# AdaLN transformer block: modulation rows computed for four partitions and repeated by DMA

## The reference

```python
mod = (_silu(L0_c) @ L0_wmod).reshape(4, 6, 1, -1)
sa, ca, ga, sb, cb, gb = (mod[:, 0], mod[:, 1], mod[:, 2], mod[:, 3], mod[:, 4], mod[:, 5])
ga = (2 * (ga >= 0) - 1) * jnp.maximum(jnp.abs(ga), 0.25)
gb = (2 * (gb >= 0) - 1) * jnp.maximum(jnp.abs(gb), 0.25)
h = _layernorm(x) * (1 + ca) + sa
x = x + ga * attention(h)          # 16 heads of 128, rope, capped scores, causal
h = _layernorm(x) * (1 + cb) + sb
x = x + gb * experts(h)            # 64 experts, top 6 in 3 of 8 groups, plus a shared one
```

## Time and profile before

| | us |
|---|---|
| median of 3 runs | 1132.64 |
| lowest and highest of the runs | 1129.94, 1132.98 |
| profiled execution, its own time | 1128.71 |
| span of its instructions | 1127.0 |
| TensorE busy in the span | 1030.5 (91%) |
| VectorE busy | 613.1 (54%) |
| ScalarE busy | 496.4 (44%) |
| GpSimd busy | 408.3 (36%) |

### The profile page before, as it was taken

The page is one execution under the profiler, slowest core; times in us unless marked ns, Lnnn a source line. Parts: engine busy times, 40 slices in busy tenths (PEclk is TensorE's granted clock), DMA queues, the critical chain, the costliest instruction groups (busy, mean ns, idle before and its releaser), DMA issues.

```text
span 1127.0 us, 17346 instructions
## 1 busy us (share of the span) xinstructions
PE 1030.5 (91%) x5813; PEld 857.0 (76%) x5813; DVE 613.1 (54%) x1424; ACT 496.4 (44%) x909; POOL 408.3 (36%) x598
## 2 busy tenths in 40 slices
PE   4999999999999999999999999999897887777774
PEld 3689989899899898998998998988564544444443
DVE  3575555657667757657865757674573211111116
ACT  1355555555555545555555565455321232223220
POOL 2232222223224555222546422265335244444440
PEclk9999999999999999999999999999999999999995
DMA  9970000001000110100101012000011598899966
GB/s 358 341 240 0 0 0 1 1 1 38 1 1 24 49 53 19 38 1 1 42 35 38 9 38 83 1 15 19 1 57 33 155 228 220 224 227 230 228 122 223
DMA packets 58752, 95.66 MB, mean 85 GB/s; under 512 B 7771, under 2 KB 41318, under 8 KB 58176
## 3 DMA queue, kind: packets, MB, share of 16 engines
q1 hardware_dynamic: 46880, 80.66, 22.4%
q0 software_dynamic: 11808, 14.16, 6.6%
HBM read 62.17 MB, written 40.67 MB: 91 GB/s over the span
## 4 chain that ended last, share of the span: by engine, by line
PE 76%; DMA 11%; DVE 7%; issue 2%; another core or an unknown queue 1%; ACT 1%; POOL 1%; SPq 1%; DVEq 0%; POOLq 0%; ACTq 0%
PE ps L1169 23%; PE ps L1216 12%; PE ps L1192 12%; PE ps L1205 10%; DMA wds<-in_wd 10%; PE ps L1382 5%; PE ps L1397 3%; PE ps L1178 2%; PE ps L1199 2%; PE ps L1181 2%; PE ps L1253 1%; PE ps L1328 1%; DMA css<-in_cossin 1%; PE ps L1150 1%
## 5 line engine op out<-in xcount | busy, mean ns | idle before, releaser
L395 POOL TENSOR_TENSOR holdp<-neghalf 128x1 f32<-128x1 f32 x145 | 31.5, 217 | 492.5 <-DVE ss L771 280.6
L550 ACT ACTIVATE prob<-ps,rn 128x512 f32<-128x512 f32 (+3 forms) x256 | 120.9, 525 | 150.6 <-PE ps L1192 150.1
L1169 PE MATMUL ps<-wh,hth 128*128 128x384 f32 x512 | 177.3, 346 | 6.2 <-DVE wl L725 6.2
L771 DVE TENSOR_REDUCE ss<-arena 128x8 f32<-128x1024 f32 x64 | 78.1, 1221 | 189.2 <-ACT arena L527 189.1
L1169 PE MATMUL ps<-wh,htl 128*128 128x384 f32 x512 | 171.9, 336 | 0.0
L1169 PE MATMUL ps<-wl,hth 128*128 128x384 f32 x512 | 171.9, 336 | 0.0
L527 ACT ACTIVATE arena<-ps 128x1024 f32<-128x1024 f32 x64 | 65.5, 1023 | 210.3 <-PE ps L1169 210.3
L1216 PEld LDWEIGHTS ps<-vx,prob 128*128 128x128 f32 x1280 | 152.9, 191 | 4.0 <-POOL prob L442 0.8
L1216 PE MATMUL ps<-vx,prob 128*128 128x129 f32 (+1 forms) x1280 | 153.4, 274 | 0.4 <-POOL prob L442 0.4
L1192 PE MATMUL ps<-qt,kt 128*128 128x512 f32 (+3 forms) x512 | 149.4, 435 | 1.9 <-DVE rows L765 1.6
L506 POOL DMA_INDIRECT acc<-wos,arena x64 | 90.2, 1409 | 139.9 <-ACT wos L661 94.3
(11 more groups left out here) (164 smaller groups left out, 1603.9 us busy)
## 6 DMA issues: line engine op xcount, KB each, us to landing
wgus<-in_wgu SPq DMA_DIRECT2D x64, 352.0 KB
wds<-in_wd SPq DMA_DIRECT2D x64, 176.0 KB
slot_rows<-pay SPq DMA_DIRECT2D x1, 7728.0 KB, 35.3
arena<-slot_rows SPq DMA_DIRECT2D x64, 120.8 KB, 3.1
warena<-in_wqkv SPq DMA_DIRECT2D x1, 4992.0 KB, 20.6
acc<-zrow SPq DMA_DIRECT2D x2, 2048.0 KB, 29.3
warena<-acc SPq DMA_DIRECT2D x8, 512.0 KB, 7.5
wos<-in_wo SPq DMA_DIRECT2D x1, 2048.0 KB, 28.9
```

What stands on the lines that cost most here:

```text
L550: act_(prob[:, OFF[j]:OFF[j] + w], sflat[:, OFF[j]:OFF[j] + w], ACT.Tanh, scale=rn[:, bass.ds(head(n), 1), TT + j:TT + j + 1].squeeze(1)). ...
L771: nc.vector.tensor_reduce(ss[:].rearrange("p (c i) -> p i c", c=2), sq, X, ALU.add).then_inc(s["ss_rdy"], 1)
L1169: last = mm(ps[:, i, 0:3 * DH], hp[:, k, i * P:(i + 1) * P], wp[:, k, :], start=(k == 0 and m == 0), stop=(k == KC - 1 and m == 2))
```

## The change

The weights of the modulation come in two transfers, the columns of the first shift and scale ahead of the first heads' weights, the other four behind them. `scb` and its two copies are gone. `mod_rows()` is called once, with the 4 columns of silu(c) as stationary operand, so that its 4 matmuls of 512 columns give all rows on 4 partitions (one per sequence). One copy takes them out of PSUM, five small operations on 4 partitions add one to the scale and clamp both gates, and SyncE writes them out to DRAM (`mod_d`, 64 KB) and reads them back to all 128 partitions (2 MB). TensorE now waits for one copy before period 0. `weights_low(0, 0)` stands ahead of `h_modulated(0)` on VectorE.

```diff
-            sp.dma_start(wmods, wmod).then_inc(s["ld_wmod"], 16)
+            sp.dma_start(wmods[:, :, 0:2 * D], wmod[:, :, 0:2 * D]).then_inc(s["ld_wmod"], 16)
             sp.dma_start(wq[:, :, 0:nf, :], wqkv[:, :, 0:nf, :]).then_inc(s["ld_wq0"], 16)
+            sp.dma_start(wmods[:, :, 2 * D:6 * D], wmod[:, :, 2 * D:6 * D]).then_inc(s["ld_wmod2"], 16)
...
+            sp.wait_ge(s["mrow_rdy"], 1)
+            sp.dma_start(mod_d, mrow).then_inc(s["mrow_out"], 16)
+            sp.wait_ge(s["mrow_out"], 16)
+            sp.dma_start(rows[:].rearrange("p b c d -> p (b c d)"),
+                         mod_d.rearrange("b c d -> (b c d)").unsqueeze(0).to_broadcast([P, B * 4 * D])).then_inc(s["rows_in"], 16)
...
-            for k in range(KC):
-                cp(scb[:, k], sc[:, k].unsqueeze(2).to_broadcast([P, B, P])).then_inc(s["scb_rdy"], 1)
-            def rows_out(b):
+            def rows_out():
-                v.wait_ge(s["rows_ps"], b + 1)
-                bk = 4 + 2 * (b % 2)
-                cp(rows[:, b], ps[:, bk:bk + 2, :].rearrange("p a (u d) -> p (a u) d", d=D)).then_inc(s["rows_sb"], 1)
+                v.wait_ge(s["rows_ps"], 1)
+                cp(mrow, ps[0:B, 4:6, :].rearrange("p a (u d) -> p (a u) d", d=D)).then_inc(s["rows_sb"], 1)
...
+            def rows_signed():
+                v.wait_ge(s["rows_sb"], 1)
+                ts(mrow[:, 2, :], mrow[:, 2, :], 1.0, None, ALU.add).then_inc(s["clamp"], 1)
+                ts(sign, mrow[:, 0:4:3, :], 0.0, 2.0, ALU.is_ge, ALU.mult).then_inc(s["clamp"], 1)
+                nc.vector.scalar_tensor_tensor(out=mrow[:, 0:4:3, :], in0=mrow[:, 0:4:3, :], scalar=-1.0, in1=mrow[:, 0:4:3, :],
+                                               op0=ALU.mult, op1=ALU.max).then_inc(s["clamp"], 1)
+            def rows_clamped():
+                v.wait_ge(s["clamp"], 3)
+                ts(mrow[:, 0:4:3, :], mrow[:, 0:4:3, :], 0.25, None, ALU.max).then_inc(s["clamp"], 1)
+                v.wait_ge(s["clamp"], 4)
+                nc.vector.scalar_tensor_tensor(out=mrow[:, 0:4:3, :], in0=sign, scalar=-1.0, in1=mrow[:, 0:4:3, :],
+                                               op0=ALU.add, op1=ALU.mult).then_inc(s["mrow_rdy"], 1)
...
-                    if p == 0:
-                        v.wait_ge(s["rows_sb"], B)
-                        ts(rows[:, :, 2, :], rows[:, :, 2, :], 1.0, None, ALU.add).then_inc(s["cb_rdy"], 1)
-                    clamp_gate(p, (0, 3)[p])
+                    rows_signed() if p == 0 else rows_clamped()
...
             ln_norm(0, 0)
+            weights_low(0, 0)
             h_modulated(0)
             h_low(0)
-            weights_low(0, 0)
...
-            rows_out(0)
-            rows_out(1)
+            rows_out()
...
-            rows_out(2)
-            rows_out(3)
...
-            v.wait_ge(s["cb_rdy"], 1)
+            v.wait_ge(s["rows_in"], 16)
...
-            def mod_rows(b):
+            def mod_rows():
+                pe.wait_ge(s["ld_wmod2"], 16)
                 for h in range(2):
                     for k in range(KC):
-                        last = mm(ps[:, 4 + 2 * (b % 2) + h, :], scb[:, k, b, :], wmods[:, k, 2 * D + h * T:2 * D + (h + 1) * T],
+                        last = mm(ps[0:B, 4 + h, :], sc[:, k, :], wmods[:, k, 2 * D + h * T:2 * D + (h + 1) * T],
                                   start=(k == 0), stop=(k == KC - 1))
...
-            pe.wait_ge(s["scb_rdy"], KC)
-            mod_rows(0)
-            mod_rows(1)
+            mod_rows()
             qk_t(0, 0)
             qkv(0, 1)
-            pe.wait_ge(s["rows_sb"], 2)
-            mod_rows(2)
-            mod_rows(3)
-            pe.wait_ge(s["rows_sb"], B)
+            pe.wait_ge(s["rows_sb"], 1)
```

More of the change, by code:

```diff
@@ L74, in build @@
         acc_d = [nc.dram_tensor(f"acc{a}", (NTOK, D), F32, kind="Internal").ap() for a in range(NACC)]
+        mod_d = nc.dram_tensor("mod_rows", (B, 4, D), F32, kind="Internal").ap()
         o95_d = nc.dram_tensor("last_rows", (E, D), F32, kind="Internal").ap()
@@ L118, in build @@
         wmods = part(KC * 6 * D).rearrange("p (k n) -> p k n", k=KC)
-        scb = part(KC * B * P).rearrange("p (k b m) -> p k b m", k=KC, b=B)
-        rat = [at[0] - KC * 6 * D - KC * B * P]
+        mrow = part(4 * D)[0:B].rearrange("p (c d) -> p c d", c=4)
+        sign = part(2 * D)[0:B].rearrange("p (c d) -> p c d", c=2)
+        rat = [at[0] - KC * 6 * D - 6 * D]
         def again(shape, dt=F32):
@@ L206, in build @@
         zrow = sb("zrow", [P, D])
-        names = """ld_x0 ld_wq0 ld_x ld_c ld_wmod ld_small ld_wqkv ld_wo ld_gate ld_sh consts fills zeros tables
-            silu_c scb_rdy modt_ps rows_ps modt_sb rows_sb clamp cb_rdy g_rdy
+        names = """ld_x0 ld_wq0 ld_x ld_c ld_wmod ld_wmod2 ld_small ld_wqkv ld_wo ld_gate ld_sh consts fills zeros tables
+            silu_c modt_ps rows_ps modt_sb rows_sb clamp mrow_rdy mrow_out rows_in g_rdy
             wh_rdy wl_rdy h_full h_high stats aggr var_eps rstd_rdy xn_rdy hmod xt_ps ht_rdy h2t_out h2_out logit_ps
```

## The result

The changed kernel took 1126.68 us in the median of 7 runs, the kernel before 1131.65 us beside it; the ratio is 0.9961 with a 95% interval of 0.9946 to 0.9976, that is 2.7 to 6.1 us less, 4.4 in the middle. One of the seven executions took 2694.81 us; it has no profile, no other run did this, and it is left out of the ratio. The profiled execution took 1126.75 us with a span of 1125.0. The prediction said 1126.0, with a gain of 6.6.

What follows compares the result with a forecast made beforehand. TensorE, busy 1030.5 of 1127.0 us, was the bound, so an earlier steady period counts in full. 0.88 - 0.20 + 1.57 + 5.62 + 0.44 = 8.3, less 1.7 for the clock: 6.6 gained, 1126.0 us, range 1122.0 to 1129.5.

Steps and rivals of the forecast that it cites:

- The last 1065 us as long as before: Sign for the profile after: the last 1065 us of the execution keep their length.
- The front: Up to `qkv(0, 0)`: moved low weights gain 0.88 us, the split delays `css` by 0.20, earlier `wmod` gains nothing.
- rival 3: Front and copies: `css` 1.0 us late, `rows_out` or copies 1 to 2 late; gain 4 to 5; 0.11 with rival 5.
- First `mod_rows`: Between `qkv(0, 0)` and `qk_t(0, 0)`: fewer matmuls, `qk_t(0, 0)` then waits for the scaled queries; gain 1.57 us.
- Second `mod_rows` and the copies: From `qkv(0, 1)` to `qk_t(0, 1)`: matmuls and `rows_out` wait leave, the norm's 5.27 us remain; gain 5.62 us.
- Clamps: VectorE in period 0: three short operations end before head 2's squares exist; gain 0.44 us.
- The way through DRAM: SyncE's write and read of the rows: in at about 90 us, covered by about 80 us, cost nothing.
- The clock: TensorE's waits before `qk_t(0, 0)` and `qk_t(0, 1)`: first keeps the clock, second costs one fall, 1.7 us; chance 0.48.
- rival 1: Neither TensorE wait in the head costs the clock: gain 8.3, 1124.3 us; chance 0.24.
- rival 2: Both TensorE waits in the head cost the clock: gain 4.9, 1127.7 us; chance 0.13.
- rival 4: Rows from DRAM late, VectorE stands after period 11: 1142 us if 100 us late; 0.04 with other outweighing losses.
- rival 5: TensorE: 4-column rows take as long as 128-column ones; gain 5.1, 1127.5 us; chance 0.11 together with rival 3.

Runs made afterwards that it cites:

- x4: The kernel before with only `weights_low(0, 0)` moved ahead of `h_modulated(0)`; ratio 1.0001 to the kernel before.
- x10: The changed kernel with both parts of `wmod` issued one behind the other, ahead of the first heads' weights; ratio 0.9957 to the kernel before.
- x6: The changed kernel with extra `mod_rows` calls as filler on TensorE, restoring 16 + 16 matmul instructions at the two places; ratio 1.0004 to the kernel before.
- x7: The kernel before without `clamp_gate`, the gates used unclamped; ratio 1.0017 to the kernel before.
- x9: The kernel before run again unedited, as a control; ratio 0.9998.
- x3: The changed kernel with the second part of `wmod` issued behind the two small tables; median 1123.22 us, ratio 0.9937 to the kernel before.
- x11: x3 run once more, unedited; median 1119.09 us, ratio 0.9949 to the kernel before.
- x12: The kernel before with `wmod` in two transfers, the second behind the small tables, nothing else; ratio 0.9981 to the kernel before.
- x1: The changed kernel run again unedited; median 1127.13 us, ratio 0.9981 to the kernel before.

## Why the prediction was right, step by step

The places and mechanisms were right: the matmuls off the chain, the norm of the next head as the next bound, the rows covered. That the time is so close (1126.68 for 1126.0) is luck twice over. First, 6.6 us were taken off a median of 1132.64; beside the changed kernel the kernel before had 1131.65, and the medians differ by 5.0 us (4.4 by the ratio). The base was 1.0 too high and the gain 1.6 too high, which leaves 0.7. Second, the 6.65 us of the head agree with 6.6 because the fall of 1.7 us that I charged did not come and the steps gave 6.65 instead of 8.3. The profiled execution shows it plainly: forecast 1122.1, measured 1126.75. "The last 1065 us as long as before" failed there; from `qk_t(0, 2)` to the end of the span it was 1065.2 and is 1069.8.

1. *The front.* Gain 0.88 for the low weights is right (0.9 to 1.0 in x4). The delay of `css` was put at 0.20 and bounded at 1.0; it was 1.2. The step that failed is the price of the split: I counted packets only (0.2, and 0.4 by x10) and took the order of equal bytes as free, which it isn't. Net the front is 0.16 us later instead of 0.68 earlier. That was the first half of rival 3 (at 0.11 together with another); its second half, late copies, did not occur.
2. *First `mod_rows`.* Forecast 1.57. From the first matmul to `qk_t(0, 0)` it took 11.40 us instead of 12.66: 1.26. The scaled queries were the next bound, as said. Of the 0.3 us that are missing, 0.1 is the first projection (6.06 instead of 5.95 us); 0.16 is that the transposes, in the timeline, had begun before the last matmul of the rows was done (34.85 there, 35.01 in the chain), which behind a wait they cannot do.
3. *Second `mod_rows` and the copies.* Forecast 5.62. From `qk_t(0, 0)` to `qk_t(0, 1)` 10.73 instead of 15.96: 5.23. Here 0.2 of the rest is that the transposes behind the wait take 0.66 instead of 0.44 us of the chain, and 0.1 that the projection takes 4.30 instead of 4.20. x6 shows that the matmuls themselves carry about 5.1 of the 6.5 us of steps 2 and 3.
4. *Clamps.* Forecast 0.44; 0.32 in the changed kernel, where `qk_t(0, 1)` starts behind a wait and takes 0.16 longer (0.95 us to the first matmul of `qkv` instead of 0.79), 0.46 alone (x7). The thin cover of the query copy held.
5. *The way through DRAM.* Forecast in by 90 us, landed at 86.2, no wait: cost nothing.
6. *The clock.* I charged 1.7 us for a fall in the second wait. In the profile it did not fall, in four of eight it did. So the mechanism is real and the length of a wait does not decide alone: 3.19 us kept the level four times, and 2.32 us had cost it. The right term was a chance, 0.8 us on the mean. The Trainium skill (TensorE: Matmul & The Clock Gate, "The HAM clock gate (the 'warmup' mystery)") says that the number of slow matmuls at the start varies from run to run of one kernel. The traces agree: 10 and 14 in the kernel before and x9, 11 and 15 in x3 and x11.

7. *The other rivals.* No fall (rival 1) is what the profile shows and four of eight do; two falls (rival 2) came in none, since the first wait was always harmless. The rows came in time (rival 4 did not occur), and eight matmuls of 4 columns took 3.60 us, none of the others remaining (rival 5 did not occur either).

8. *Figures that were wrong.* The rows written to DRAM are 16 KB, not 64; since the read is 2 MB either way, the time is the same. The lowest case less half the spread is 1124.3 - 1.5 = 1122.8, not 1122.0. And with 80 us of cover, rows 100 us late would cost 20 us, 1146 and not 1142. None of these bears on the result.

The terms measured, -0.16 + 1.26 + 5.23 + 0.32, make the 6.65 us of the head; forecast without the clock were 8.3. What I did not have is the part that is given back later. 0.4 us is VectorE standing at 569.78 ahead of the normalisation for sequence 3 (L714), behind nothing that the profile shows; TensorE then waits 0.4 us at the scores in period 12 of sequence 2. The changed kernel, then x7:

```profile
573.98 2.40 PE L1195 MATMUL ps<-qt,kt 128*128 128x512 f32 x8 [0.41 <-DVE arena L795]
```

```profile
581.22 2.40 PE L1191 MATMUL ps<-qt,kt 128*128 128x512 f32 x8 [0.42 <-DVE arena L790]
```

VectorE's idle time there is 2.08 us in all nine profiles with 4-partition rows and also in x7, which has the old rows without the clamps, and 1.71 or 1.72 us in the four profiles that clamp on 128 partitions. So it is no chance and does not come from the rows: it goes with taking `clamp_gate` out of VectorE's instructions. Why that costs 0.4 us 500 us later is open. 1.0 us is the fall of the clock at the last projection of head outputs (L1208): it shows in six of nine profiles with 4-partition rows and one of five with 128-partition rows, too few to say that the change causes it. The 0.9 us of the router's tail have no cause shown. The 2.3 us of the expert stretch may be spread from run to run, as x12 with the old rows had the longest stretch, but that is not shown. The profile before was itself a short one (1128.71 us, median 1131.65), which is why the two spans differ by 2.0 us and the medians by 5.0.

## What to carry to other kernels

Matmuls that make 128 equal rows are worth replacing by one small product and a broadcasting transfer where they stand on TensorE's chain and the result is needed late; their price is then their whole duration, less the part that covered another engine's chain. After such a cut look at what the transfers' order does to the smallest table in the queue: here putting the late 1024 KB behind it gave 2.45 us on the head, beside 6.65 for the whole change. What a head gains need not reach the end: of these 6.65 us the times show 4.4 in one comparison and 2.1 in the other. And charge a fall of the clock as a chance times its price when a wait of some microseconds opens.

## What the runs showed of the hardware

- A wait of the same length, 3.19 us, kept TensorE's higher level in four profiles and lost it in four. In x1 the level fell 1.7 us after the matmuls had begun again.
- The matmuls of the first projection reached the closer spacing of the higher level 2.7 us after the first of them in x1 and x4, 3.3 in the kernel before, 5.0 in x11 and 5.6 in x12.
- With the same bytes ahead of it, the small table was taken at 12.68 to 13.02 us in the six profiles with `wmod` whole or in 6 KB pieces, and at 13.90 to 14.33 in the three with the change's order.
- The kernel before ran 4.3 to 5.5 us faster on one chip than on the two others. The expert stretch of its profile there was the same (210.7); the difference, 59.7 us instead of 64.5, lies between the last layer norm's transposes and the first expert. It is one wait of TensorE and the clock behind it: 1.41 us and 5.46 us of matmuls in x9, where the earlier trace rows have 4.65 and 7.08. All four profiles from that chip (x9 to x12) have a wait of 1.40 or 1.41 us there, the other ten 2.83 to 4.74 us.

```profile
869.40 5.46 PE L1328 MATMUL ps<-wos,warena 128*128 128x256 f32 x24 [1.41 <-DVE warena L807]
```
